# The gate weights load in twelve pieces, the first batches are turned in another order, and the last output tiles get buffers of their own

## The chip, the cores and the metric

The kernel runs on one core of one Trainium2 chip. The metric is the device time of one execution in microseconds (us). Three runs of the kernel before gave a median of 959.32 us (958.61 to 961.28).

## The reference

The input `x` is 32 batches of 128 rows by 512 columns. Each batch has a category; its 512 x 512 matrix and its bias are picked from 64. What follows is a gated feed-forward network with simulated quantisation:

```
c    = x @ W[cat] + b[cat]                       # per batch
c    = act_qdq(c)                                # 16-bit scale from max|c| over everything
up   = act_qdq(c @ lpbq(w_up).T)                 # 512 -> 1536
gate = act_qdq(c @ lpbq(w_gate).T)
gate = act_qdq(gate * u16(sigmoid(gate)))
o    = act_qdq(gate * up)
out  = x + o @ lpbq(w_down).T                    # 1536 -> 512
```

`lpbq` rounds weights to 4 bits with one scale for each block of 32 along the inner dimension. `act_qdq` needs the maximum over the whole tensor, so each stage must be complete before the next can be quantised.

## The kernel before, in words

Every engine has its instructions written out by hand; they meet at semaphores. The 32 batches are 8 chunks of 4 (`BPC`); in what follows a batch is numbered 0 to 31 and `r` is its place in its chunk.

**Conditioning stage (the first 139 us).** For each batch PE turns `x` with four transposes (`turn_x`, L750), ACT copies the result out of PSUM into `xt` (`copy_xt`, L537), PE multiplies with the batch's matrix in `w_ring` (`cond_matmul`, L760), and DVE adds the bias (`add_bias`, L1018). PE turns batch b+1 just ahead of multiplying batch b. `x_ring` and `w_ring` have four places each, so SP may issue the matrix of batch b (1 MB) only when the product of batch b-4 is done, and right behind it the `x` of batch b+1 (256 KB). Batches 0 and 1 are multiplied in halves of the contraction (`cond_halves`, L779), since their matrices come in two loads. Between the halves of batch 0 PE sums up the biases of all batches (eight small instructions into `bias_bank`) and turns batch 1 (`sum_bias_and_turn`, L812). Thirteen matmuls on zeros (`spare_matmuls`) fill PE's time before the first matrix is there.

**Weights beside it.** SP also loads `w_gate` into `wf` in four loads of 768 KB, behind the matrices of batches 7, 8, 9 and 11 (`load_chunk`, L393). DVE takes the maximum of each block of 32 of such a quarter (`gate_blocks`, L1055): quarter 0 after batch 11, quarters 1, 2, 3 after batches 12, 13, 14. `weight_steps` (three instructions, L977) follows after batch 14, and `weight_scale` (seven instructions on one column, L983) after batch 15; its last one signals `wscale_ready`. From chunk 4 on DVE quantises one slice of 512 columns ahead of each `add_bias` (`quantise_slice`, L1001, three instructions). ACT makes the upper part of each slice (`high_part`, L545). In chunk 4 ACT's order is: copy batch 16, copy batch 17, wait for `wscale_ready`, `high_part(0)`, copy batch 18, `high_part(1)`, copy batch 19, `high_part(2)` (`cond_chunk` of ACT, L569). ACT works strictly in this order, and PE's product of batch 18 needs the copy of batch 18.

**Gate and up projections, elementwise work, maxima.** From 142 to 644 us PE multiplies all chunks with both weights in float16 high and low parts; then DVE and ACT find the maximum of the product.

**Down projection (from 700 us).** Chunks alternate between two sets of four PSUM banks. PE multiplies a chunk in four quarters (`down_quarter`, L912), in each for four tiles `r`, each with nine matmuls of 512 columns. DVE finishes a tile (`finish_tile`, L1391: scale, and add `x` from `x_res`) into `y_out`; both have two places. SP stores it and loads the next `x_res` behind that (`finish_chunk`, L496). At the end SP waits for the stores to land.

## Time and profile before

| what | us |
|---|---|
| median of three runs | 959.32 |
| profiled execution, its own time | 959.35 |
| its span, first to last instruction | 957.5 |
| PE busy | 894.5 |
| DVE busy | 657.7 |
| ACT busy | 420.6 |
| conditioning stage, PE | 1.2 to 139 |
| PE idle between up and down projection | 643.7 to 700.0 |
| last matmul starts | 953.68 |

The profile lists for each engine when an instruction started and what ended the idle time ahead of it. The chain of waits goes back from the last instruction to whatever released each step; work on it counts one to one in the time, all else is hidden. PE has few idle stretches: 1.2 us at the start, 0.6 us ahead of the first product, three tenths at 142 us and the long one at 644 us. The duration of a matmul in a row contains the time until its result has drained, so rows overlap; the distance between starts is what a matmul costs in a stream.

### The profile page before, as it was taken

To read this page: it belongs to the slowest core of one execution; us is meant where nothing else is said; L and a number is where in the kernel's file an instruction comes from. 1 tells how busy PE (TensorE), PEld (TensorE's weight loads), DVE (VectorE), ACT (ScalarE), POOL (GpSimd) and SP (SyncE) were. 2 spreads that over 40 slices of the span, in tenths; PEclk is the share of its full clock that TensorE was granted. 3 is DMA by queue.
4 is the path that set the end of the run, shared out by engine and by line. 5 is a ranking of instruction groups with operands and counts; after the bars stand their busy time and mean duration, and the time that the engine had idled before them with its cause. 6 is when DMAs were issued, how large, how long until landed. Compare 5 with 4: busy or idle time off the path is not lost.

```text
span 957.5 us, 13113 instructions
## 1 busy us (share of the span) xinstructions
PE 894.5 (93%) x4736; PEld 477.7 (50%) x4736; DVE 657.7 (69%) x792; ACT 420.6 (44%) x454; POOL 3.1 (0%) x12
## 2 busy tenths in 40 slices
PE   9999999999999999999999999980079999999998
PEld 7999994444444444444444444430034444444443
DVE  2349869655667455279898889669999878855511
ACT  1112335223223232299798882229866444444000
POOL 0000000000000000000000000000000000000000
PEclk9999999999999999999999999995579999999999
DMA  9999862553574443689999735999978999977221
GB/s 334 405 393 325 324 242 100 165 164 122 165 253 131 141 132 121 220 304 419 407 388 391 261 125 207 407 422 414 418 272 317 320 339 348 331 272 282 88 88 66
DMA packets 81587, 254.32 MB, mean 266 GB/s; under 512 B 32082, under 2 KB 32082, under 8 KB 77714
## 3 DMA queue, kind: packets, MB, share of 16 engines
q1 hardware_dynamic: 46354, 198.72, 55.5%
q10 hardware_dynamic: 35200, 55.20, 16.4%
q8 instruction: 15, 0.25, 0.1%
q14 instruction: 18, 0.15, 0.0%
HBM read 173.94 MB, written 73.66 MB: 259 GB/s over the span
## 4 chain that ended last, share of the span: by engine, by line
PE 90%; DMA 4%; ACT 3%; issue 1%; DVE 1%; SPq 0%; ACTq 0%; POOL 0%; DVEq 0%
PE bank L857 16%; PE bank L858 16%; PE bank L859 16%; PE bank L771 11%; PE bank L892 6%; PE bank L894 6%; PE bank L893 6%; ACT umag L701 2%; DMA up_extra<-up_scratch 2%; PE bank L757 2%; PE bank L904 1%; PE bias_bank L892 1%; PE wt_bank L892 1%; PE wt_bank L893 1%; PE wt_bank L894 1%
## 5 line engine op out<-in xcount | busy, mean ns | idle before, releaser
L607 ACT ACTIVATE stage<-bank 128x512 f32<-128x512 f32 x186 | 108.5, 593 | 212.3 <-PE bank L859 161.2
L1135 DVE TENSOR_REDUCE tile_max<-stage 128x1 f32<-128x1536 f32 (+1 forms) x62 | 108.4, 1748 | 34.7 <-ACT stage L607 31.7
L857 PE MATMUL bank<-xq_head,wt_up 128*128 x336 | 127.4, 379 | 0.9 <-ACT stage L607 0.9
L857 PE MATMUL bank<-xq_head,wt_gate 128*128 (+1 forms) x336 | 127.4, 379 | 0.3 <-DVE xq_head L1122 0.3
L858 PE MATMUL bank<-xq_head,wt_up 128*128 x336 | 127.3, 379 | 0.0
L859 PE MATMUL bank<-xq_head,wt_up 128*128 x336 | 127.3, 379 | 0.0
L858 PE MATMUL bank<-xq_head,wt_gate 128*128 (+1 forms) x336 | 127.3, 379 | 0.0
L859 PE MATMUL bank<-xq_head,wt_gate 128*128 (+1 forms) x336 | 127.3, 379 | 0.0
L771 PE MATMUL bank<-xt,w_ring 128*128 128x128 f32 x960 | 112.1, 275 | 0.0
L771 PEld LDWEIGHTS bank<-xt,w_ring 128*128 128x128 f32 x960 | 109.9, 192 | 0.0
L1015 DVE SCALAR_TENSOR_TENSOR wparts<-wf,scal,wparts 128x512 f16<-128x512 f32 (+2 forms) x36 | 27.0, 749 | 62.9 <-ACT wparts L550 62.8
L1397 DVE SCALAR_TENSOR_TENSOR y_out<-bank,scal,x_res 128x512 f32<-128x512 f32 x24 | 17.9, 747 | 69.3 <-PE bank L894 66.8
L893 PE MATMUL bank<-wt_down,o_even 128*128 128x512 f16 x168 | 63.7, 379 | 0.0
L892 PE MATMUL bank<-wt_down,o_even 128*128 128x512 f16 x168 | 63.7, 379 | 0.0
L894 PE MATMUL bank<-wt_down,o_even 128*128 128x512 f16 x168 | 63.7, 379 | 0.0
L929 PE MATMUL bank<-wt_down 128*128 128x512 f16 x11 | 4.9, 630 | 56.3 <-DVE o_max L1329 56.3
L649 ACT ACTIVATE code<-gate_ring,scal 128x1536 int16<-128x1536 f32 x32 | 50.2, 1571 | 11.7 <-DMA wt_down<-wparts 6.8
L1329 DVE CUSTOM_DVE_ANT_0 junk<-act_codes,umag 128x1536 bf16<-128x1536 int16 x32 | 53.9, 1755 | 1.3 <-ACT umag L701 1.3
L1377 DVE SCALAR_TENSOR_TENSOR ocode<-act_codes,scal,ocode 128x1536 int16<-128x1536 int16 x30 | 54.3, 1810 | 0.4
L720 ACT ACTIVATE ocode<-up_ring,scal 128x1536 int16<-128x1536 f32 x31 | 48.4, 1561 | 11.6 <-DVE o_odd_head L1387 7.0
L857 PEld LDWEIGHTS bank<-xq_head,wt_up 128*128 128x128 f16 x336 | 32.9, 98 | 41.0 <-ACT stage L607 1.4
L857 PEld LDWEIGHTS bank<-xq_head,wt_gate 128*128 128x128 f16 x336 | 32.9, 98 | 40.4 <-DVE xq_head L1122 1.3
(205 smaller groups left out, 1354.4 us busy)
## 6 DMA issues: line engine op xcount, KB each, us to landing
up_ring<-up_scratch SPq DMA_DIRECT2D x54, 768.0 KB, 7.4
w_ring<-in_L_cond_W_dram SPq DMA_DIRECT2D x30, 1024.0 KB, 6.6
gate_scratch<-stage ACTq DMA_DIRECT2D x32, 768.0 KB, 3.4
gate_ring<-gate_scratch SPq DMA_DIRECT2D x32, 768.0 KB, 9.4
up_scratch<-stage ACTq DMA_DIRECT2D x30, 768.0 KB, 7.9
product_scratch<-prod_ring SPq DMA_DIRECT2D x19, 768.0 KB, 9.0
back_ring<-product_scratch SPq DMA_DIRECT2D x19, 768.0 KB, 13.0
gate_even<-gate_scratch SPq DMA_DIRECT2D x16, 768.0 KB, 8.0
```

Source lines behind the costliest of these rows:

```text
L607: nc.scalar.activation(stage[:, q % 2, n % PIECE_TILES, :], up_bank(i, n), ACT.Copy)\
L649: nc.scalar.activation(code[:, j % 2, :], gate_ring[:, j % RING, :], ACT.Copy, scale=k_g)\
L771: mm = nc.tensor.matmul(bank[:, m * S:(m + 1) * S], w_ring[:, r, k, m * P:(m + 1) * P], xt[:, r % 2, k, :], start=(k == 0), stop=(k == KH ...
L857: nc.tensor.matmul(bank, w_hi, x_hi, start=(k == 0), stop=False)
L858: nc.tensor.matmul(bank, w_hi, x_lo, start=False, stop=False)
L859: mm = nc.tensor.matmul(bank, w_lo, x_hi, start=False, stop=(k == KH - 1))
L892: nc.tensor.matmul(bank, o_hi, wt_down[:, 0, k, :], start=(k == 0), stop=False)
L893: nc.tensor.matmul(bank, o_hi, wt_down[:, 1, k, :], start=False, stop=False)
L894: return nc.tensor.matmul(bank, o_lo, wt_down[:, 0, k, :], start=False, stop=(k == NT - 1))
L1135: V.tensor_reduce(tile_max[:, side, bass.ds(Q * i + q, 1)], stage[:, q % 2, :, :].rearrange("p t c -> p (t c)"), AX.X, ALU.max, apply_abso ...
L1329: V.tensor_tensor_reduce(junk[:, k % 2, :], act_piece(max_piece(k)), umag[:, k % MSLOTS, :], 1.0, 0.0, ALU.mult, ALU.max, o_max[:, k:k + 1 ...
L1377: V.scalar_tensor_tensor(out=ocode[:, q % 2, :], in0=act_piece(n), scalar=k_o, in1=ocode[:, q % 2, :], op0=ALU.mult, op1=ALU.mult).then_in ...
```

## The change

Four things change.

1. `w_gate` is loaded in twelve loads of 256 KB, one behind the matrix of each of the batches 6 to 17 (`GATE_AT = 6`); each quarter has a semaphore. The loops over chunks 1 to 4 on SP are written out for this.
2. DVE takes the maxima of quarter 0 after batch 7, of quarter 1 after batch 10, of quarter 2 after batch 13, and of quarter 3 after batch 15. `weight_steps` follows behind quarter 3, after batch 15, and `weight_scale` after batch 16.
3. PE does the bias sum and the turn of batch 1 right behind the turn of batch 0, ahead of the first half of batch 0. The spare matmuls are nine, then three (eight, then five before). `halves_copied` now counts two copies, so that each of two PSUM banks is waited for by itself.
4. The last two output tiles have their own `x_tail` and `y_tail`, loaded by one 512 KB load well ahead. The last tile is computed as two halves of 256 columns in two banks (`last_quarter`): per quarter eighteen matmuls of 256 columns in the place of nine of 512. DVE finishes and SP stores each half by itself. PE's loop over pairs of chunks is one round shorter and the last two chunks are written out.

```diff
+GATE_AT = 6
...
+        x_tail = place("x_tail", R + 30 * K, [2, H], f32)
+        y_tail = place("y_tail", R, [2, H], f32)
...
-                    if r in gate_parts:
-                        at = SLICES * gate_parts[r]
-                        sp.dma_start(wf[:, at:at + SLICES, :], wg_view[:, at:at + SLICES, :]).then_inc(wgate_in, 16)
-
-            load_chunk(1, {3: 0})
-            load_chunk(2, {0: 1, 1: 2, 3: 3})
-            with sp.Fori(3, CHUNKS) as i:
-                load_chunk(i, {})
+                    if isinstance(i, int) and 0 <= BPC * i + r - GATE_AT < WSLICES:
+                        n = BPC * i + r - GATE_AT
+                        sp.dma_start(wf[:, n, :], wg_view[:, n, :]).then_inc(wgate_in[n // SLICES], 16)
+
+            for i in range(1, 5):
+                load_chunk(i)
+            with sp.Fori(5, CHUNKS) as i:
+                load_chunk(i)
...
+            sp.wait_ge(sgn_made, PIECES - 1)
+            sp.dma_start(x_tail[:, :, :], x_flat[B - 2:B, :, :].rearrange("a s d -> s a d")).then_inc(xtail_in, 16)
             finish_chunk(CHUNKS - 1, 0, True)
+            for n, (b, cols) in enumerate(((B - 2, slice(0, H)), (B - 1, slice(0, H // 2)), (B - 1, slice(H // 2, H)))):
+                sp.wait_ge(ytail_made, n + 1)
+                sp.dma_start(out[b, :, cols], y_tail[:, b - B + 2, cols]).then_inc(ytail_out[n], 16)
...
             pe.wait_ge(spare_made, 1)
-            spare_matmuls(8)
+            spare_matmuls(9)
...
-                        if r and m == 2:
-                            pe.wait_ge(halves_copied, 1)
+                        if r and m >= 2:
+                            pe.wait_ge(halves_copied, m - 1)
...
-                cond_halves(0, sum_bias_and_turn)
+                sum_bias_and_turn()
+                spare_matmuls(3)
+                cond_halves(0, None)
...
             turn_x(0, 0, True)
-            spare_matmuls(5)
             first_cond_chunk()
...
+                for half, bank in enumerate((down_bank(1, BPC - 1), down_bank(0, 0))):
+                    cols = slice(half * H // 2, (half + 1) * H // 2)
+                    for t in range(PIECE_TILES):
+                        k = PIECE_TILES * q + t
+                        o_hi, o_lo = (o_slot(1, q)[:, part, t, (BPC - 1) * P:BPC * P] for part in range(2))
+                        nc.tensor.matmul(bank[:, cols], o_hi, wt_down[:, 0, k, cols], start=(k == 0), stop=False)
+                        nc.tensor.matmul(bank[:, cols], o_hi, wt_down[:, 1, k, cols], start=False, stop=False)
+                        mm = nc.tensor.matmul(bank[:, cols], o_lo, wt_down[:, 0, k, cols], start=False, stop=(k == NT - 1))
+                    if q == Q - 1:
+                        mm.then_inc(right_done if half else left_done, 1)
...
             def in_chunk_3(r):
-                if r < 3:
-                    gate_blocks(r + 1)
-                if r == 2:
+                if r == 1:
+                    gate_blocks(2)
+                if r == 3:
+                    gate_blocks(3)
                     dve.wait_ge(wblocks_maxed, KH)
                     weight_steps(0, WG)
-                if r == 3:
-                    weight_scale(0, WG)
-
-            cond_chunk(1)
-            cond_chunk(2, None, lambda r: gate_blocks(0) if r == 3 else None)
+
+            cond_chunk(1, None, lambda r: gate_blocks(0) if r == 3 else None)
+            cond_chunk(2, None, lambda r: gate_blocks(1) if r == 2 else None)
             cond_chunk(3, None, in_chunk_3)
-            cond_chunk(4, 2)
+            cond_chunk(4, 2, lambda r: weight_scale(0, WG) if r == 0 else None)
...
+            for half, bank in enumerate((down_bank(1, BPC - 1), down_bank(0, 0))):
+                cols = slice(half * H // 2, (half + 1) * H // 2)
+                dve.wait_ge(right_done if half else left_done, 1)
+                V.scalar_tensor_tensor(out=y_tail[:, 1, cols], in0=bank[:, cols], scalar=k_y, in1=x_tail[:, 1, cols],
+                                       op0=ALU.mult, op1=ALU.add).then_inc(ytail_made, 1)
```

At the start of the program, behind the first spare matmul, PE's rows before the change are these (`spare` are the zeros, `ident` with `x_ring` a turn, `bias_rows` the bias sum, `w_ring` a product; in brackets stands what is waited for):

```order
L744 MATMUL bank<-spare 128x512 x7
L757 MATMUL bank<-ident_93,x_ring 128x128 [waits x_in0,ident_made]
L757 MATMUL bank<-ident_93,x_ring 128x128 x3
L744 MATMUL bank<-spare 128x512 x5
L792 MATMUL bank<-xt,w_ring 128x128 [waits w_head_in0,x_copied]
L792 MATMUL bank<-xt,w_ring 128x128 x5
L792 MATMUL wt_bank<-xt,w_ring 128x128 x2
L815 MATMUL bias_bank<-onehot,bias_rows 128x32 [waits onehot_made]
L815 MATMUL bias_bank<-onehot,bias_rows 128x32 x3
L757 MATMUL bank<-ident_93,x_ring 128x128 [waits x_in1]
L757 MATMUL bank<-ident_93,x_ring 128x128 x3
L792 MATMUL bank<-xt,w_ring 128x128 [waits w_in0]
```

And these are PE's rows at the start of the changed kernel:

```order
L758 MATMUL bank<-spare 128x512 [waits spare_made]
L758 MATMUL bank<-spare 128x512 x8
L771 MATMUL bank<-ident_95,x_ring 128x128 [waits x_in0,ident_made]
L771 MATMUL bank<-ident_95,x_ring 128x128 x3
L829 MATMUL bias_bank<-onehot,bias_rows 128x32 [waits onehot_made]
L829 MATMUL bias_bank<-onehot,bias_rows 128x32 x3
L771 MATMUL bank<-ident_95,x_ring 128x128 [waits x_in1]
L771 MATMUL bank<-ident_95,x_ring 128x128 x3
L758 MATMUL bank<-spare 128x512 x3
L806 MATMUL bank<-xt,w_ring 128x128 [waits w_head_in0,x_copied]
L806 MATMUL bank<-xt,w_ring 128x128 x5
L806 MATMUL wt_bank<-xt,w_ring 128x128 x2
```

The four bias instructions and the turn that waits for `x_in1` stood between the two halves of batch 0 (`w_head_in0` and `w_in0`); now they stand ahead of both, with three spare matmuls behind them.

On DVE, at the end of chunk 3 before the change (`wstep` to `wrecip` are the weight steps, `scal` on one column is the scale, `cond_head` is a bias addition, that of batch 15 here, `cond_max` the maximum of a chunk):

```order
L979 TENSOR_SCALAR wstep<-wstep 128x192 [waits wblocks_maxed]
L980 RECIPROCAL wrecip<-wstep 128x192 [waits scalar_step]
L981 TENSOR_REDUCE scal<-wstep 128x1 [waits scalar_step]
L1029 TENSOR_TENSOR cond_head<-bank,bias 128x4x128 [waits cond_done]
L987 TENSOR_SCALAR scal<-scal 128x1 [waits all_max]
L988 TENSOR_SCALAR scal<-scal 128x1 [waits scalar_step]
L989 TENSOR_SCALAR scal<-scal 128x1 [waits scalar_step]
L990 TENSOR_SCALAR scal<-scal 128x1 [waits scalar_step]
L991 TENSOR_SCALAR scal<-scal 128x1 [waits scalar_step]
L993 TENSOR_SCALAR scal<-scal 128x1 [waits scalar_step]
L995 COPY scal<-scal 128x1 [waits scalar_step]
L1045 TENSOR_REDUCE cond_max<-cond_head 128x1 [waits cond_copied]
```

And DVE from the maxima of quarter 3 on in the changed kernel, where the first bias addition is that of batch 16:

```order
L1101 TENSOR_REDUCE wstep<-wf 128x48 [waits wgate_in3]
L1022 TENSOR_SCALAR wstep<-wstep 128x192 [waits wblocks_maxed]
L1023 RECIPROCAL wrecip<-wstep 128x192 [waits scalar_step]
L1024 TENSOR_REDUCE scal<-wstep 128x1 [waits scalar_step]
L1088 TENSOR_REDUCE cond_max<-cond_head 128x1 [waits cond_copied]
L1048 TENSOR_TENSOR wf<-wf,wrecip 128x512
L1050 TENSOR_SCALAR wf<-wf 128x512 [waits w_scaled]
L1052 TENSOR_TENSOR wf<-wf,wstep 128x512 [waits w_rounded]
L1072 TENSOR_TENSOR cond_head<-bank,bias 128x4x128 [waits cond_done]
L1030 TENSOR_SCALAR scal<-scal 128x1 [waits all_max]
```

The weight steps moved behind batch 15, and the scale moved past the chunk's maximum, the quantising of slice 0 and the bias addition of batch 16.

## Rows read from the trace of the kernel before

**Rows 1.** The page, the chain that ended last, by engine:

```profile
PE 90%; DMA 4%; ACT 3%; issue 1%; DVE 1%; SPq 0%; ACTq 0%; POOL 0%; DVEq 0%
```

**Rows 2.** Timeline, PE, from 1 us (start us, length us, engine, line, operation):

```profile
1.16 3.60 PE L744 MATMUL bank<-spare 128*128 128x512 f16 x8 [1.16 <-DVE spare L955]
...
4.84 1.10 PE L757 MATMUL bank<-ident,x_ring 128*128 128x128 f32 x4
...
5.74 1.46 PE L744 MATMUL bank<-spare 128*128 128x512 f16 x5
```

**Rows 3.** Chain that ended last, to 25 us (start us, us until the next):

```profile
7.83 1.58 PE bank L792 x12
...
9.86 1.00 PE bias_bank L815 x8
...
11.54 1.34 PE bank L792 x12
...
19.80 3.57 PE bank L771 x32
```

**Rows 4.** Tile w_ring, the load of batch 3, issued at 8.58 us:

```profile
DMA to landing us min/median/max: 11.3/11.3/11.3
```

**Rows 5.** Chain that ended last, 47 to 56 us:

```profile
50.02 0.48 PE bank L757 x4
...
54.14 0.74 PE bank L757 x4
```

**Rows 6.** Tile x_ring, loads issued from 40 to 60 us:

```profile
DMA to landing us min/median/max: 7.0/9.4/10.7
```

**Rows 7.** DMA view, 40 to 60 us:

```profile
DMA packets 2250, 8.21 MB, mean 410 GB/s; under 512 B 192, under 2 KB 192, under 8 KB 1600
```

**Rows 8.** Timeline, DVE, 71 to 82 us:

```profile
71.26 1.74 DVE L1058 TENSOR_REDUCE wstep<-wf 128x48 f32<-128x1536 f32 x1
73.03 0.26 DVE L979 TENSOR_SCALAR wstep<-wstep 128x192 f32<-128x192 f32 x1
...
74.98 0.68 DVE L1029 TENSOR_TENSOR cond_head<-bank,bias 128x512 f32<-128x512 f32 x1
75.58 0.14 DVE L987 TENSOR_SCALAR scal<-scal 128x1 f32<-128x1 f32 x1
...
76.77 2.28 DVE L1045 TENSOR_REDUCE cond_max<-cond_head 128x1 f32<-128x2048 f32 x1
78.96 0.68 DVE L1005 TENSOR_TENSOR wf<-wf,wrecip 128x512 f32<-128x512 f32 x1
...
80.75 0.68 DVE L1029 TENSOR_TENSOR cond_head<-bank,bias 128x512 f32<-128x512 f32 x1
```

**Rows 9.** Timeline, ACT, 80 to 82 us:

```profile
80.93 0.72 ACT L550 ACTIVATE wparts<-wf,scal 128x512 f16<-128x512 f32 x1 [5.15 <-DVE wf L1009]
81.56 0.58 ACT L542 ACTIVATE xt<-bank 128x512 f32<-128x512 f32 x1
```

**Rows 10.** Timeline, PE: turn of batch 17, product of batch 18:

```profile
74.50 0.64 PE L757 MATMUL bank<-ident,x_ring 128*128 128x128 f32 x4
...
83.09 3.74 PE L771 MATMUL bank<-xt,w_ring 128*128 128x128 f32 x32
```

**Rows 11.** Timeline, PE, the last matmul:

```profile
953.68 0.38 PE L894 MATMUL bias_bank<-wt_down,o_odd_tail 128*128 128x512 f16 x1
```

**Rows 12.** Chain that ended last, from 951 us:

```profile
951.43 2.73 DMA x_res<-in_x_dram
...
954.24 0.75 DVE y_out L1397
```

**Rows 13.** Timeline, DVE, a bias addition of 128 columns out of PSUM:

```profile
13.44 0.35 DVE L1023 TENSOR_SCALAR cond_head<-bank,bias 128x128 f32<-128x128 f32 x1 [2.25 <-PE wt_bank L792]
```

**Rows 14.** Windows (us, busy of PE, PEld, DVE, ACT, POOL; granted clock; DMA; GB/s):

```profile
647.00:648.00 1.00, 0.00 (x0) 0.00 (x0) 0.69 (x1) 1.00 (x2) 0.00 (x0) 0.93 1.02 418
...
705.00:706.00 1.00, 1.00 (x4) 0.39 (x3) 0.93 (x3) 0.00 (x0) 0.00 (x0) 0.55 1.00 406
```

More of the change, by code:

```diff
@@ L269, in sem @@
             return ctx.enter_context(nc.semaphore(name))
-        idx_in, bias_in, wgate_in, wup_in = sem("idx_in"), sem("bias_in"), sem("wgate_in"), sem("wup_in")
+        idx_in, bias_in, wup_in = sem("idx_in"), sem("bias_in"), sem("wup_in")
+        wgate_in = [sem(f"wgate_in{m}") for m in range(KH)]
         w_in = [sem(f"w_in{n}") for n in range(BPC)]
@@ L316, in adaln_ffn @@
         y_out_done = [sem(f"y_out_done{n}") for n in range(2)]
+        xtail_in, ytail_made = sem("xtail_in"), sem("ytail_made")
+        ytail_out = [sem(f"ytail_out{n}") for n in range(3)]
+        left_done, right_done = sem("left_done"), sem("right_done")
         ky_made = sem("ky_made")
@@ L391, in _, with load_chunk @@
                     load_x_batch(0, r + 1, True)
[L393 removed]
+            def load_chunk(i):
                 for r in range(BPC):
@@ L496, in finish_chunk @@
             def finish_chunk(i, pairs_left, last):
-                for r in range(BPC):
+                for r in range(BPC // 2 if last else BPC):
                     if r < pairs_left:
@@ L508, in finish_chunk @@
                                  y_out[:, r % 2, :]).then_inc(y_out_done[r % 2], 16)
-                    if not last or r < 2:
+                    if not last:
                         load_x(BPC * i + r + 2, r)
@@ L515, in _ @@
             finish_chunk(CHUNKS - 2, 0, False)
+            sp.wait_ge(sgn_made, PIECES - 1)
+            sp.dma_start(x_tail[:, :, :], x_flat[B - 2:B, :, :].rearrange("a s d -> s a d")).then_inc(xtail_in, 16)
             finish_chunk(CHUNKS - 1, 0, True)
+            for n, (b, cols) in enumerate(((B - 2, slice(0, H)), (B - 1, slice(0, H // 2)), (B - 1, slice(H // 2, H)))):
+                sp.wait_ge(ytail_made, n + 1)
+                sp.dma_start(out[b, :, cols], y_tail[:, b - B + 2, cols]).then_inc(ytail_out[n], 16)
             for r in range(2):
-                sp.wait_ge(y_out_done[r], 16 * B // 2)
+                sp.wait_ge(y_out_done[r], 16 * (B - 2) // 2)
+            for n in range(3):
+                sp.wait_ge(ytail_out[n], 16)
         @block.gpsimd
@@ L922, in down_quarter, with last_quarter @@
                     mm.then_inc(piece_used, 1)
+            def last_quarter(q):
+                pe.wait_ge(o_ready, PIECES - Q + q + 1)
+                for r in range(BPC - 1):
+                    if q == 0:
+                        pe.wait_ge(y_made, BPC * (CHUNKS - 3) + r + 1)
+                    for t in range(PIECE_TILES):
+                        mm = down_tile(1, q, r, t)
+                    if q == Q - 1:
+                        mm.then_inc(out_done, 1)
+                if q == 0:
+                    pe.wait_ge(y_made, BPC * (CHUNKS - 2) + 1)
+                for half, bank in enumerate((down_bank(1, BPC - 1), down_bank(0, 0))):
+                    cols = slice(half * H // 2, (half + 1) * H // 2)
+                    for t in range(PIECE_TILES):
+                        k = PIECE_TILES * q + t
[3 more added lines that the diff above has]
+                        mm = nc.tensor.matmul(bank[:, cols], o_lo, wt_down[:, 0, k, cols], start=False, stop=(k == NT - 1))
+                    if q == Q - 1:
+                        mm.then_inc(right_done if half else left_done, 1)
+                if q < Q - 1:
+                    mm.then_inc(piece_used, 1)
             for j in range(SLICES):
@@ L935, in _ @@
                         down_quarter(h, h, q, True)
-            with pe.Fori(1, CHUNKS // 2) as pair:
+            with pe.Fori(1, CHUNKS // 2 - 1) as pair:
                 for h in range(2):
@@ L939, in _ @@
                         down_quarter(2 * pair + h, h, q, False)
+            for q in range(Q):
+                down_quarter(CHUNKS - 2, 0, q, False)
+            for q in range(Q):
+                last_quarter(q)
         @block.vector
@@ L1424, in _ @@
             down_pair(CHUNKS // 2 - 1, False, True)
-            for h in range(2):
-                for r in range(BPC):
-                    finish_tile(CHUNKS - 2 + h, r, h, False)
+            for r in range(BPC):
+                finish_tile(CHUNKS - 2, r, 0, False)
+            for r in range(2):
+                finish_tile(CHUNKS - 1, r, 1, False)
+            dve.wait_ge(out_done, B - 1)
+            dve.wait_ge(xtail_in, 16)
+            V.scalar_tensor_tensor(out=y_tail[:, 0, :], in0=down_bank(1, 2), scalar=k_y, in1=x_tail[:, 0, :],
+                                   op0=ALU.mult, op1=ALU.add).then_inc(ytail_made, 1)
[3 more added lines that the diff above has]
+                V.scalar_tensor_tensor(out=y_tail[:, 1, cols], in0=bank[:, cols], scalar=k_y, in1=x_tail[:, 1, cols],
+                                       op0=ALU.mult, op1=ALU.add).then_inc(ytail_made, 1)
 _INS = ['x', 'itok_B_0_63', 'L0_cond_W', 'L0_cond_b', 'L0_ffn_w_gate', 'L0_ffn_w_up', 'L0_ffn_w_down']
```

5 lines of the change are left out of this document (2 added, 3 removed).

## The prediction

> **What bounds the kernel now.** I read the page's chain first: PE holds 90% of it [rows 1], so what counts is where PE is later or earlier than its own stream of instructions. Then the timeline and the chain at both ends of the program, the landing of the loads that PE turns and multiplies, and DVE and ACT around 71 to 84 us, since the change touches these. The reader is to see four things. At the start PE's own work sets the time from 7.83 us on [rows 3]. In the conditioning stage a batch costs PE 4.05 us (0.48 for a turn, 3.57 for 16 matmuls as 32 rows of f32 halves) [rows 3, 5], and everything else hides behind it, once excepted [rows 5]. ACT's copy of batch 18 is only 0.95 us ahead of PE: it ends at 81.56 + 0.58 = 82.14, PE needs it at 83.09 [rows 9, 10]. And after the last matmul [rows 11] the rest is serial: one wait for a load, a DVE instruction, a store [rows 12].
>
> **Part 1, the start.** Between the halves of batch 0 stand the bias sum and a turn, 9.86 to 11.54: 1.68 us go from there [rows 3]. They now stand ahead. Eight spare matmuls from 1.16 took 3.60, so 0.45 each, and a ninth moves the turn of batch 0 from 4.84 to about 5.05. That turn issues in 0.90 (to 5.74) [rows 2]: 5.95. The bias sum adds 1.00, the turn of batch 1 the 0.68 left of the 1.68 [rows 3]: 7.63. Three spare matmuls at about 0.22 (five took 1.46 with a slow first one and the drain [rows 2]) give 8.28, against 7.83: 0.45 later. In return the first half of batch 0, 2.03 us before (7.83 to 9.86), should take 1.79, half of the 3.57 of a full batch [rows 3], since PE no longer idles ahead of it: 0.24. Sum: 1.68 - 0.45 + 0.24 = 1.47 us gained. Bounds: nothing, if the moved work runs on the slow clock of the first microseconds or a load is late; 1.9 if all of it fits ahead of 7.83. The split of `halves_copied` lets PE wait for one DVE copy instead of two; a copy lasts 0.35 [rows 13], of which I count nothing. What is late next is the matrix of batch 3: issued at 8.58, landed 11.3 later at 19.88 [rows 4]. Its product began 1.79 behind 19.80, at 21.59 [rows 3], and would now begin at 20.12. That just fits.
>
> **Part 2, the gate loads.** Before, the `x` of batch 12 was issued at 43.28 behind three megabytes of gate weights and took 10.7 us [rows 6], to 53.98. PE's turn at 54.14 came 4.12 after the last one at 50.02 and took 0.74 instead of 0.48 [rows 5]: 0.07 + 0.26 = 0.33 us lost, which the spread loads give back. At that point only six slices (1.6 MB) instead of 3.1 MB have gone ahead; at 410 GB/s [rows 7] that is 3.8 us less queue, while PE comes 1.8 earlier. One batch (1.31 MB) with one slice (0.26 MB) takes 3.85 us at 410 GB/s [rows 7] against PE's 4.05, so the queue does not grow. The eight more DMA issues on SP stand ahead of the next `x` load each time; SP waits for PE in every batch, and that wait hides them. Bounds: 0.33 gained; nothing gained.
>
> The Trainium skill's page "DMA: Bandwidth & Descriptors" (Bandwidth, Measured) asks for DMAs of 1 MiB or more and so speaks against cutting four loads into twelve; its fit in Anatomy of one DMA has about 2 us of fixed cost each. Laid end to end that would make a batch with its slice longer than PE's 4.05, and PE would wait. The trace has 256 KB loads mixed with 1 MB ones at 410 GB/s [rows 7], so the costs overlap here and I give this little weight (a rival below).
>
> **Part 3, the weight scale.** This is the dearest part. Times are from the end of batch 15's product, E = 74.50 before [rows 10]. Turns are 4.05 apart, so that of batch 16 was at 70.45, and DVE's maxima at 71.26 [rows 8] came 0.81 behind the product's end (bias addition in between). DVE in the changed order: maxima of quarter 3 start at E + 0.81; +1.77 (71.26 to 73.03) weight steps; +1.95 (to 74.98) chunk maximum; +2.19 (76.77 to 78.96) quantise slice 0; +1.79 (to 80.75) add bias 16; +0.60 (74.98 to 75.58) scale; +1.19 (to 76.77) and 0.08 to its end [rows 8]: `wscale_ready` at E + 10.38. Before, it came at about E + 2.35, and ACT waited for slice 0 instead, to E + 6.43 = 80.93 [rows 9]. ACT then needs 0.10 to start, 0.63 for `high_part(0)` and 0.58 for the copy of batch 18 [rows 9]: E + 11.69, with a hop to PE 11.75. PE wants it at 83.09 - 74.50 = 8.59 [rows 10]. So PE stands idle for 3.16 us. Behind ACT's wait are queued the copies of batches 18 and 19; the second comes at about E + 13.4, PE asks for it at 11.75 + 4.05, so it costs nothing more. DVE reaches bias 18 when PE has finished it, as before, and from there the stage has its old rhythm; nothing gives the 3.16 back, since the end of the stage is again PE. Slice 11 goes out behind the matrix of batch 17, when batch 13's product ends: E - 8.10, 64.6 with the 1.8 us gained so far, and 0.7 for SP's three issues, 65.3; with the 7.0 us that the last load of rows 6 took it is there by 72.5, DVE asks at 74.50 - 1.80 + 0.81 = 73.5. Bounds: 2.2 (if the DVE steps close up) to 4.5 (if slice 11 is a microsecond late). That the earlier maxima (after batches 7, 10, 13) move into idle time of DVE is free.
>
> **Part 4, the end.** PE's stream ends as before; eighteen matmuls of 256 columns per quarter for nine of 512 may add a few nanoseconds each, 0.08 in all (an estimate; bounds 0 to 0.3). The last tile waited for `x_res`: issued 951.43, 2.73 on the way, 954.16 [rows 12], while PE was done at 953.68 + 0.38 = 954.06 [rows 11]; with `x_tail` loaded long ahead 0.10 goes. DVE's 0.75 for 512 columns [rows 12] and 0.35 for 128 [rows 13] give 0.48 for 256: 0.27 less. The left half runs under PE's right half. The last store carries 131 KB less, 0.32 at 410 GB/s [rows 7]. Together 0.10 + 0.27 + 0.32 - 0.08 = 0.61 gained; bounds 0.1 (the store's time is all latency) and 0.8.
>
> **Sum.** 959.35 (the profiled execution, practically the median 959.32) - 1.47 - 0.33 + 3.16 - 0.61 = 960.1 us.
>
> **Rivals.** *A, no stall*: ACT or DVE gets there in time and the gains stand alone: 959.35 - 1.47 - 0.33 - 0.61 = 956.9. For it: the sum of parts 1, 2, 4 is solid; against it: seven DVE steps in a fixed order with measured lengths, and ACT's strict order. 11%. *B, the clock falls in the stall* (the slower side): PE stopped at 643.7, and the granted clock was 0.93 in the mean of 647 to 648, so it fell at about 647.9, 4.2 us later; PE began again at 700.0, and the mean of 0.55 from 705 to 706 says it was back at 705.9 [rows 14]. 5.9 us at 1.2 instead of 2.4 GHz cost 3.0: 963.1. It decides if the clock has fallen by the time the copy of batch 18 is there; my stretch is 3.2 us, shorter than the 4.2 of that row, which speaks against. 13%. The Trainium skill warns, in "TensorE: Matmul & The Clock Gate" (Why this matters for your kernels), against idle gaps of a few microseconds between bursts of matmuls; by that rule B would be the likelier case. *C, nothing gained at the start*: clock late for the moved work, or batch 3's matrix late: 961.5. 10%. *D, the twelve loads are too slow* and PE waits for them, 0.2 us or more in each of twelve batches: 962.5 and above. 4%. The forecast has 62%.
>
> **How the numbers follow.** A measurement of this kernel tells about 0.3%, 2.9 us, from no change: faster is below 956.4, slower above 962.2. The forecast's own range, from the bounds that are likely together, is 959.0 to 961.3: no change. A lies at the edge inside, and somewhat under half of it (with the upper bounds of parts 1 and 4) below: faster 6 to 8%. B mostly and D are slower: 14%. The range that holds 8 in 10 takes in most of A and the near part of B: 956.8 to 962.6.
>
> **What would show it.** `wscale_ready`'s copy instruction at 83.0 or so; ACT's `high_part(0)` waiting for that instruction and no longer for L1009's successor; an idle stretch of about 3 us of PE ahead of batch 18 with the copy as releaser, and a granted clock of 1.00 behind it. Batch 3's product at 20.1; no longer turn at batch 12; a last DVE instruction of about 0.48. The prediction is wrong if PE has no gap near 81 us, if the clock falls there, or if PE waits for a load at 16 to 20 us.

## The result, and the profile after it

| | before | changed |
|---|---|---|
| median of 11 executions, same comparison | 960.60 us | 962.67 us |
| lowest to highest | 958.61 to 961.41 | 962.19 to 964.10 |
| profiled execution (its span) | 959.35 (957.5) | 962.19 (960.3) |
| its mean granted clock | 0.970 | 0.970 |

The medians differ by 2.07 us. The ratio of the two kernels is 1.0025, with a 95% interval of 1.0015 to 1.0035, which is 2.4 us: slower, and the interval leaves no change out. The forecast was 960.1, 0.75 above its base of 959.35, and called no change, with a range up to 962.6. The measured 962.67 lies just above that range. Of the 2.57 us between forecast and measured time 1.25 are not the change's: in this comparison the kernel before itself took 960.60 and not 959.35. The other 1.3 us are what the change cost more than forecast, and they are what has to be explained.

First the profiled execution. Its chain that ended last (start us, us until the next) up to 25 us, which answers to [rows 3]:

```profile
3.75 7.88 DMA w_ring<-in_L_cond_W_dram
...
11.68 1.60 PE bank L806 x12
...
19.98 0.48 PE bank L771 x4
20.46 3.57 PE bank L785 x32
```

The full product that began at 19.80 before begins at 20.46: the start is 0.66 us later, not 1.47 earlier. PE had done its early work in time. Its timeline (start us, us, engine, line, operation, idle before and releaser):

```profile
1.16 4.02 PE L758 MATMUL bank<-spare 128*128 128x512 f16 x9 [1.16 <-DVE spare L998]
...
5.27 1.04 PE L771 MATMUL bank<-ident,x_ring 128*128 128x128 f32 x4
...
6.34 1.07 PE L829 MATMUL bias_bank<-onehot,bias_rows 64*128 64x32 f32 x8
```

What came late is a load: the second half of batch 0's matrix was issued at 3.75 and landed 7.88 us later. In the traces of the kernel before and of all experiments below it took 5.1 to 6.0 us. So this is something of this execution and not of the change, and the experiments have to say what the start is worth. PE waited 1.2 us for it, which is about half of what this execution lost at the start: in e4, the same code there, this product begins at 18.32, 2.14 earlier. The rest is no single wait.

PE's own waits (engine, line, waited for: us in total, times, longest) show that load and the stall that part 3 of the prediction described:

```profile
PE bank L785 <- ACT xt L556: 3.0, 1, 3.0
...
PE bank L806 <- DMA w_ring<-in_L_cond_W_dram: 1.2, 1, 1.2
```

The timeline of DVE, which answers to [rows 8]:

```profile
74.98 0.69 DVE L1072 TENSOR_TENSOR cond_head<-bank,bias 128x512 f32<-128x512 f32 x1 [3.36 <-PE bank L785]
75.58 1.74 DVE L1101 TENSOR_REDUCE wstep<-wf 128x48 f32<-128x1536 f32 x1
77.36 0.26 DVE L1022 TENSOR_SCALAR wstep<-wstep 128x192 f32<-128x192 f32 x1
...
79.31 2.27 DVE L1088 TENSOR_REDUCE cond_max<-cond_head 128x1 f32<-128x2048 f32 x1
81.51 0.68 DVE L1048 TENSOR_TENSOR wf<-wf,wrecip 128x512 f32<-128x512 f32 x1
...
83.29 0.68 DVE L1072 TENSOR_TENSOR cond_head<-bank,bias 128x512 f32<-128x512 f32 x1
83.89 0.14 DVE L1030 TENSOR_SCALAR scal<-scal 128x1 f32<-128x1 f32 x1
...
85.01 0.15 DVE L1038 COPY scal<-scal 128x1 f32<-128x1 f32 x1
```

ACT, which answers to [rows 9], and PE, which answers to [rows 10]:

```profile
85.20 0.72 ACT L564 ACTIVATE wparts<-wf,scal 128x512 f16<-128x512 f32 x1 [9.14 <-DVE scal L1038]
85.83 0.58 ACT L556 ACTIVATE xt<-bank 128x512 f32<-128x512 f32 x1
```

```profile
74.78 0.64 PE L771 MATMUL bank<-ident,x_ring 128*128 128x128 f32 x4
...
82.88 0.64 PE L771 MATMUL bank<-ident,x_ring 128*128 128x128 f32 x4
86.53 3.83 PE L785 MATMUL bank<-xt,w_ring 128*128 128x128 f32 x32 [3.01 <-ACT xt L556]
```

E, the time of 74.50 before, is 74.78 here. The scale is ready at 85.16, E + 10.38, and the product of batch 18 starts at E + 11.75: both to the hundredth as forecast. In this execution the granted clock stayed up behind the gap (window from 86 us; us, busy of PE, PEld, DVE, ACT, POOL; granted clock; DMA share; GB/s):

```profile
86.00:87.00 1.00, 0.47 (x4) 0.48 (x5) 0.96 (x3) 0.42 (x2) 0.00 (x0) 1.00 1.08 422
87.00:88.00 1.00, 1.00 (x12) 1.00 (x11) 1.00 (x2) 1.00 (x2) 0.00 (x0) 1.00 0.89 352
```

At the end, which answers to [rows 11, 12], PE and DVE:

```profile
957.36 0.27 PE L957 MATMUL bank<-wt_down,o_odd_tail 128*128 128x256 f16 x1
957.67 0.48 DVE L1478 SCALAR_TENSOR_TENSOR y_tail<-bank,scal,x_tail 128x256 f32<-128x256 f32 x1 [0.50 <-PE bank L957]
```

From the start of the last DVE instruction to the end of the span it is 2.63 us now and was 3.26 (957.5 - 954.24).

The balance of the two profiled executions, read at the same three places: the start +0.66 (20.46 - 19.80); from there to E -0.38 (74.78 - 74.50 is 0.28), the longer turn and waits of batches 10 and 12 that are gone; from E to the product of batch 18 +3.16 (86.53 - 83.09 is 3.44); the rest -0.60. Together +2.84, which is 962.19 - 959.35.

That balance explains this one execution, and not the median. It had the clock at 0.970 on average, which is the highest of the 11 (four have it), and a late load by chance. The other seven executions had a mean clock of 0.966 or 0.968. In 107 undisturbed executions of the kernel before, run beside the experiments, one was below 0.970. So the first theory is: **the stall of 3 us lets TensorE's clock fall in most executions** (rival B of the prediction), and parts 1, 2 and 4 gain what was forecast. The main rivals: part 1 gains nothing, because the first matrix comes late (SP's loop written out, or the loads' order); and the twelve loads cost time by themselves.

### The profile page after: what moved, and what is told of

Read it like the earlier page. It is cut to its first block, busy times and chain, and to the rows that moved or that the text cites. A ratio compares the mean times of both kernels' runs of the same rounds, so it can differ in the third digit from the quotient of the medians.

```text
span 960.3 us, 13140 instructions
## 1 busy us (share of the span) xinstructions
PE 894.4 (93%) x4771; PEld 481.1 (50%) x4771; DVE 657.8 (68%) x793; ACT 420.9 (44%) x454; POOL 3.1 (0%) x12
## 4 chain that ended last, share of the span: by engine, by line
PE 89%; DMA 4%; ACT 3%; issue 2%; DVE 2%; SPq 0%; ACTq 0%; POOL 0%; DVEq 0%
PE bank L872 16%; PE bank L873 16%; PE bank L874 16%; PE bank L785 10%; PE bank L908 6%; PE bank L907 6%; PE bank L909 6%; ACT umag L715 2%; DMA up_extra<-up_scratch 2%; PE bank L771 1%; PE bank L919 1%; PE wt_bank L908 1%; PE wt_bank L907 1%; PE wt_bank L909 1%; DMA wt_down<-wparts 1%
```

## The experiments

Each time is a median, beside the median of the kernel before on the same chip. The ratios behind the times are not the quotients of these medians, and differ from them by up to 0.9 us.

### One part at a time

**e1: part 4 alone** (parts 1 to 3 undone).

```diff
-                sum_bias_and_turn()
-                spare_matmuls(3)
-                cond_halves(0, None)
+                cond_halves(0, sum_bias_and_turn)
...
-            for i in range(1, 5):
-                load_chunk(i)
-            with sp.Fori(5, CHUNKS) as i:
-                load_chunk(i)
+            load_chunk(1, {3: 0})
+            load_chunk(2, {0: 1, 1: 2, 3: 3})
+            with sp.Fori(3, CHUNKS) as i:
+                load_chunk(i, {})
```

> The kernel before with part 4 alone (own buffers for the last two tiles, the last tile in halves). Theory (the prediction's part 4): 0.6 us faster than before, 0.1 to 0.8. Rival (the store's time is all latency and the written-out chunks cost PE time): no gain, the last DVE instruction shorter by 0.27 but the span not. In the profile: last DVE instruction 0.48 us, from its end to the end of the span about 0.3 us less than before.

958.32 beside 958.86, ratio 0.9993 (0.9984 to 1.0002). The timeline at the end:

```profile
953.06 0.27 PE L955 MATMUL bank<-wt_down,o_odd_tail 128*128 128x256 f16 x1
953.37 0.48 DVE L1477 SCALAR_TENSOR_TENSOR y_tail<-bank,scal,x_tail 128x256 f32<-128x256 f32 x1 [0.50 <-PE bank L955]
```

The last two matmuls of 256 columns start 0.11 apart, so one of 512 would have started at 952.95. From there to the end of the span (956.1) it is 3.15 us, against 3.82 before (957.5 - 953.68): 0.67 gained, where the forecast has 0.61. The median's 0.5 agrees but is too small to be told from nothing.

**e2: part 1 alone** (loads of `w_gate`, DVE's order and the end as before).

```diff
-            cond_chunk(1, None, lambda r: gate_blocks(0) if r == 3 else None)
-            cond_chunk(2, None, lambda r: gate_blocks(1) if r == 2 else None)
+            cond_chunk(1)
+            cond_chunk(2, None, lambda r: gate_blocks(0) if r == 3 else None)
             cond_chunk(3, None, in_chunk_3)
-            cond_chunk(4, 2, lambda r: weight_scale(0, WG) if r == 0 else None)
+            cond_chunk(4, 2)
```

> The kernel before with part 1 alone (bias sum and turn of batch 1 ahead of batch 0, nine and three spare matmuls). Theory S (the changed order itself makes PE wait for the second half of batch 0's matrix and costs what the profile after shows there): batch 3's product begins at about 22.2 us instead of 21.6, time 0.5 to 1 us above before. Rival L (the order gains 1.5 us as predicted, and the late landing in the profile after, 11.6 instead of 8.95 us, was the luck of one execution): batch 3's product at 20.1 to 20.6 us, time 1 to 1.5 us below before.

958.67 beside 958.86, ratio 1.0000 (0.9991 to 1.0009): nothing. But the chain shows the gain, and where it goes:

```profile
18.03 3.57 PE bank L777 x32
...
33.13 12.34 DMA x_ring<-in_x_dram
...
45.51 0.75 PE bank L763 x4
...
53.98 0.74 PE bank L763 x4
```

The product that began at 19.80 before begins at 18.03, 1.77 us earlier. At 45.51 the gain is nearly used up: the `x` of that batch, issued at 33.13, was 12.34 us on the way behind the gate weights, and the turn took 0.75. The turn at 53.98 stands against 54.14 in [rows 5]. An earlier start is worth nothing while the loads behind it are late. Part 2 is what turns it into time. Neither theory written down for e2 had this: one expected a later start, the other 1 to 1.5 us in the time.

**e3: parts 2 and 3 alone** (start and end as before).

```diff
-            spare_matmuls(9)
+            spare_matmuls(8)
...
-                sum_bias_and_turn()
-                spare_matmuls(3)
-                cond_halves(0, None)
+                cond_halves(0, sum_bias_and_turn)
```

> The kernel before with parts 2 and 3 alone (twelve loads of 256 KB, maxima and scale moved). Theory (the stall of part 3 behind ACT's wait for the weight scale, less the wait of batch 12 that goes): +3.2 - 0.3 = 2.8 us slower than before, one gap of 3.0 to 3.3 us of PE ahead of batch 18's product. Rival (the slower start is caused by the loop over chunks 1 to 4 written out on SP or by the loads, not by the order on PE): the second half of batch 0's matrix lands at 11 us or later here too, and the time is 4 us or more above before.

964.12 beside 958.86, ratio 1.0046 (1.0032 to 1.0060), and all 5 executions below 0.970. PE's timeline and the windows:

```profile
86.03 5.44 PE L778 MATMUL bank<-xt,w_ring 128*128 128x128 f32 x32 [3.01 <-ACT xt L549]
```

```profile
86.00:87.00 1.00, 0.97 (x4) 0.97 (x5) 1.00 (x3) 0.51 (x1) 0.00 (x0) 0.51 0.96 369
...
88.00:89.00 1.00, 1.00 (x7) 1.00 (x7) 0.97 (x3) 0.13 (x1) 0.00 (x0) 0.50 0.23 96
89.00:90.00 1.00, 1.00 (x9) 1.00 (x9) 0.50 (x1) 0.59 (x1) 0.00 (x0) 0.79 0.13 49
```

Here the clock is at half, 1.2 of 2.4 GHz, from the moment PE resumes, and the product takes 5.44 us instead of the 3.83 it took without a fall. That is most of why the loss is 4.4 us (by the ratio) to 5.3 (by the medians) and not the 2.8 expected. The second half of batch 0's matrix was 5.4 us on the way although SP's loop is written out here as in the changed kernel: that rival is false.

### Taking the stall away

**e4: everything but the stall.** ACT copies batch 18 before it waits for the scale:

```diff
-                    if weights == 1 and r == 1:
-                        act.wait_ge(wscale_ready, 1)
-                    if weights is not None and r >= weights:
-                        high_part(0, BPC * (i - 4) + r - 1, BPC * (i - 4) + r - 1, 0)
+                    if weights == 1 and r == 2:
+                        act.wait_ge(wscale_ready, 1)
+                        high_part(0, 0, 0, 0)
+                    elif weights == 1 and r == 3:
+                        high_part(0, 1, 1, 0)
+                        high_part(0, 2, 2, 0)
+                    elif weights == 0:
+                        high_part(0, BPC * (i - 4) + r - 1, BPC * (i - 4) + r - 1, 0)
```

> The changed kernel with ACT's order alone altered in chunk 4: the copy of batch 18 comes ahead of the wait for the weight scale, high parts 0, 1, 2 behind the copies of batches 18 and 19. Theory (the stall is ACT's strict order): no gap of PE ahead of batch 18, 3.2 us less than the changed kernel, so about 0.8 us below the kernel before. Rival (DVE itself is too late there and PE then waits for a bias addition instead): a gap of 1 us or more ahead of batch 20, less than 2 us gained on the changed kernel.

956.26 beside 958.86, ratio 0.9973 (0.9963 to 0.9982), none of 10 executions below 0.970. Its chain:

```profile
18.32 3.57 PE bank L789 x32
...
40.37 0.48 PE bank L775 x4
...
44.42 0.48 PE bank L775 x4
...
48.48 0.48 PE bank L775 x4
...
52.53 0.48 PE bank L775 x4
```

The product of batch 3 starts at 18.32 + 1.79 = 20.11, where the prediction has 20.12, and the turns from 40 to 53 us are 4.05 or 4.06 apart: the twelve loads cost PE nothing. ACT now waits 5.10 us instead of 9.14, behind the copy:

```profile
83.06 0.72 ACT L564 ACTIVATE wparts<-wf,scal 128x512 f16<-128x512 f32 x1 [5.10 <-DVE scal L1042]
```

The prediction's rival A, all gains and no stall, is 956.9 - 959.35 = -2.4 us; e4 has -2.6. So parts 1, 2 and 4 were sized right together, and part 3 with what follows it is the whole loss. **e15** is the same kernel on another chip.

> The changed kernel with ACT's order altered, again: every execution at a mean clock of 0.970 or 0.971, ratio to before 0.9965 to 0.998, 3.2 us (the stall) below e14 and 4 to 5 below e13.

956.66 beside 958.85, ratio 0.9986 (0.9975 to 0.9997), 1 of 12 executions below 0.970. It gains less than e4 by the ratio because three executions at a mean clock of 0.970 took 959.88 to 960.12, and e7 below has two of the kind (959.80 and 959.98). None of these has a trace.

**e7: the scale earlier instead** (slices from batch 5 on, maxima and scale one batch earlier, as far as they follow from it):

```diff
-GATE_AT = 6
+GATE_AT = 5
...
+                if r == 3:
+                    weight_scale(0, WG)
...
-            cond_chunk(4, 2, lambda r: weight_scale(0, WG) if r == 0 else None)
+            cond_chunk(4, 2)
```

> The changed kernel with every slice of w_gate and its maxima one batch earlier (behind batches 5 to 16; maxima after batches 6, 9, 12, 14, steps after 14, scale after 15 as before the change). Theory (twelve loads are harmless, only the scale's place costs): no gap ahead of batch 18, 3.2 us and the clock's part less than the changed kernel, 2.6 us below before, like the kernel with ACT's order altered. Rival D (small loads crowd the queue when they begin earlier): PE waits for x or a matrix between batches 5 and 12, 0.3 us or more in sum, above the kernel with ACT's order altered.

956.45 beside 958.79, ratio 0.9981 (0.9970 to 0.9991), 0 of 12, and no gap ahead of batch 18. Two quite different edits that remove the gap give the same time.

**e10: e4 without part 1** (the edit shown for e3, made on e4).

> The changed kernel with ACT's order altered and without part 1 (bias sum and turn of batch 1 back between the halves of batch 0). Theory (part 1 is worth 1.5 us once the spread loads of part 2 let PE keep it; alone it was given back at the turns of batches 9, 10 and 12): 0.9 to 1.0 us below before (0.33 and 0.6), 1.5 us above the kernel with ACT's order altered. Rival (the gain came from parts 2 and 4, part 1 is worth nothing): the same time as with it, 2.4 us below before.

957.37 beside 958.79, ratio 0.9985 (0.9976 to 0.9995). It is 1.4 us below the kernel before, where e4 is 2.6 and e15 is 2.2 below in their medians. So part 1 is worth 1.2 or 0.8 us of the 1.47, and by the ratio of e15 (0.9986) nothing. The three ran on three chips: the medians don't settle it, and the size of part 1 rests on the traces.

**e8: e4 without the three spare matmuls** ahead of the first half batch.

```diff
                 sum_bias_and_turn()
-                spare_matmuls(3)
                 cond_halves(0, None)
```

> The changed kernel with ACT's order altered as before and without the three spare matmuls ahead of the first product. Theory: the first product begins when its half matrix is there (7.7 to 8.0 us) instead of 8.2 us: 0.2 to 0.5 us less than with them. Rival: PE's clock is no longer kept up for the first product, which then takes longer than 1.8 us: no gain or 0.5 us and more lost.

956.53 beside 958.79, ratio 0.9978 (0.9969 to 0.9987): the same as e4, where 0.2 to 0.5 us less was expected. The first product starts at 8.06 instead of 8.19, the bias sum takes 1.31 us in the place of 1.0:

```profile
6.04 1.31 PE bias_bank L833 x8
```

### A stall, but shorter or filled

**e9: DVE's chunk maximum (2.27 us) moved from ahead of the scale to behind batch 17's bias addition.**

```diff
...
-            cond_chunk(4, 2, lambda r: weight_scale(0, WG) if r == 0 else None)
+            def in_chunk_4(r):
+                if r == 0:
+                    weight_scale(0, WG)
+                if r == 1:
+                    chunk_max(3)
+
+            cond_chunk(4, 2, in_chunk_4)
```

The lines left out make chunk 3 itself leave its maximum out.

> The changed kernel with DVE's maximum of chunk 3 (2.19 us) moved from ahead of the weight scale to behind the bias addition of batch 17. Theory (DVE's steps in order, added up, set ACT's wait, and the clock falls only in a long gap): a gap of 3.0 - 2.2 = 0.8 us of PE ahead of batch 18, mean clock 0.970 or 0.971 in every execution, time 0.8 to 1.0 us above the kernel with ACT's order altered, so 1.4 to 1.8 us below before. Rival (any gap there brings the clock down): executions with a mean clock of 0.966 to 0.968 remain.

957.25 beside 958.79, ratio 0.9985 (0.9976 to 0.9994), 0 of 11 executions below 0.970:

```profile
82.57 3.61 PE L785 MATMUL bank<-xt,w_ring 128*128 128x128 f32 x30 [0.85 <-ACT xt L556]
```

With 0.85 us of gap the kernel is still faster than before. The gap has shrunk by 2.16 of the 2.27 that were moved, so the chain of DVE steps in the prediction is the one that counts.

**e6, e11, e14: PE works on zeros in the stall** (the output isn't touched; chunk 4 of PE's loop is written out for it). e6 and e14 are the same kernel, with 12 matmuls; e11 has 14.

```diff
+                    if isinstance(i, int) and i == 4 and r == 2:
+                        for _ in range(12):
+                            nc.tensor.matmul(bias_bank[:, :], spare[:, 0:P], spare[:, :], start=True, stop=True)
...
-            with pe.Fori(1, CHUNKS - 1) as i:
+            with pe.Fori(1, 4) as i:
+                cond_chunk(i, False, False)
+            cond_chunk(4, False, False)
+            with pe.Fori(5, CHUNKS - 1) as i:
```

> The changed kernel with twelve matmuls on zeros (2.6 us) in the stall ahead of batch 18's product, chunk 4 written out on PE; the stall itself stays. Theory K: the clock stays at 1.00 there in every execution, mean clock 0.970 or above throughout, time 1 to 2 us below the changed kernel and closer together. Rival R: no difference to the changed kernel, 0.3 us at most.

> The changed kernel with fourteen matmuls on zeros (3.0 us) in the stall instead of twelve. Theory K (the clock falls because PE idles): no execution below a mean clock of 0.970, 1 to 2 us below the changed kernel. Rival (what fell to 0.968 in two executions with twelve was not the stall): executions of 0.968 remain with fourteen.

> The same with the twelve matmuls on zeros in the stall. Theory K: at most two in eleven executions below 0.970, median 1 to 2 us below e13. Rival: no difference.

e6: 960.55 beside 958.79, ratio 1.0021 (1.0010 to 1.0032), 2 of 9 executions below 0.970. e11: 960.83 beside 958.79, 1.0026 (1.0014 to 1.0039), 1 of 9. e14: 960.73 beside 958.85, 1.0020 (1.0011 to 1.0028), 1 of 11. For e6 and e11 no execution below 0.970 was expected, so with filling some are left, and two more matmuls did not change that. PE in e14:

```profile
81.41 2.75 PE L851 MATMUL bias_bank<-spare 128*128 128x512 f16 x12
84.51 1.72 PE L785 MATMUL bank<-xt,w_ring 128*128 128x128 f32 x13 [0.34 <-ACT xt L556]
```

**e13: e14 without its matmuls**, the fair partner, made from it so:

```diff
-                        for _ in range(12):
+                        for _ in range(0):
```

> The changed kernel with chunk 4 written out on PE and nothing in the stall: the control to e14. Theory K (the stall brings PE's clock down in part of the executions): half or more of the executions with a mean clock below 0.970, median 1 us or more above e14. Rival (filling does nothing): same share of executions below 0.970 and the same median as e14.

963.11 beside 958.85, ratio 1.0045 (1.0029 to 1.0061), 8 of 10 below 0.970. e13 and e14 differ only in what PE does in the gap, ran on the same chip, and differ by 2.4 us, with intervals that don't overlap. Batch 18 comes at 84.57 and 84.51, so the gap is equally long: **what PE does in the gap is worth 2.4 us, and brings the executions below 0.970 from 8 of 10 to 1 of 11.** The trace of e13 shows the fall:

```profile
84.00:85.00 1.00, 0.43 (x3) 0.44 (x4) 0.96 (x3) 0.51 (x2) 0.00 (x0) 1.00 1.03 389
85.00:86.00 1.00, 1.00 (x8) 1.00 (x7) 1.00 (x3) 0.91 (x2) 0.00 (x0) 0.58 0.86 354
```

By the turn behind batch 18 (89.87 against 88.18) the fall has cost 1.7 us. So not all of the 2.4 need be the fall itself: the two traces also differ in a later wait (next sentences) and in the clock at the down projection ("A second draw", below). e14 is 1.9 us above the kernel before, where the forecast's sum with a clock that holds is 0.8. Some 0.6 of the 1.1 between stand at PE's one wait for ACT's stage copy, behind 150 us: 1.5 to 1.7 us in the filled kernels and 2.5 in e13, against 1.0 in the changed kernel and 0.9 in the kernel before (a wait that the list of idle stretches ahead of the prediction leaves out). Whether the written-out code does that wasn't followed up.

### The changed kernel again

> The changed kernel once more, as it is, beside the next three. Theory K (PE's clock falls in the 3 us stall ahead of batch 18 in part of the executions): about 2.2 us above before, executions spread over some 3 us in steps with their mean clock (0.966 to 0.970), and if the profiled one has 0.968 or less, windows at 86 to 90 us with a granted clock of 0.5. Rival R (the spread is the landing of the first matrices): the mean clock doesn't go with the time, and the first products are later in slow executions.

> The changed kernel as it is, on the same chip as the three others, since its executions spread. Theory K: 2 to 4 us above before, most executions with a mean clock of 0.966 to 0.968, these 1 to 2.5 us slower than those at 0.970. Rival: the mean clock and the time do not go together.

**e5**: 962.17 beside 958.79, ratio 1.0043 (1.0030 to 1.0056), 4 of 5 executions below 0.970. The profiled one held the clock (0.971), had no late matrix, and took 959.12: 0.3 above the median before, where the forecast says 0.8. The four others took 961.78 to 964.17. **e12**, on another chip: 960.41 beside 958.79, ratio 1.0012 (1.0002 to 1.0021), 3 of 11 below 0.970, where 2 to 4 us and most executions were expected. Its profiled execution is one of the three, and shows the fall. PE:

```profile
80.95 0.64 PE L771 MATMUL bank<-ident,x_ring 128*128 128x128 f32 x4
84.60 1.68 PE L785 MATMUL bank<-xt,w_ring 128*128 128x128 f32 x11 [3.01 <-ACT xt L556]
```

and the windows:

```profile
84.00:85.00 1.00, 0.40 (x3) 0.41 (x4) 0.96 (x3) 0.47 (x1) 0.00 (x0) 1.00 1.04 410
85.00:86.00 1.00, 1.00 (x10) 1.00 (x9) 1.00 (x3) 0.95 (x2) 0.00 (x0) 0.88 0.97 363
86.00:87.00 1.00, 1.00 (x7) 1.00 (x6) 0.93 (x3) 0.26 (x1) 0.00 (x0) 0.50 0.34 127
...
88.00:89.00 1.00, 1.00 (x6) 1.00 (x6) 0.06 (x1) 0.16 (x1) 0.00 (x0) 0.50 0.04 16
89.00:90.00 1.00, 1.00 (x10) 1.00 (x9) 0.00 (x0) 0.00 (x0) 0.00 (x0) 0.91 0.00 0
```

PE stopped at about 81.6 and was back at 84.60 with a full clock. These rows show a granted clock of 1.00 or 0.50, and means between where it changed: the mean of 0.88 from 85 to 86 us says that the clock fell at about 85.8, when PE had been busy for 1.2 us, and it came back at about 89.2. The rows show 7, 7 and 6 matmuls a microsecond where there are 10 to 12 at full clock; the product took 5.46 us in all, against 3.83 with the clock up: 1.63 lost here. In e13 the same reading gives a fall at about 85.2, 0.6 us after PE resumed, and in e3 it came as PE resumed; all three came back 3.4 us after the fall.

**A second draw at the down projection.** PE stands idle once more, from about 644 to 700 us, in every kernel here. The traces show that the clock is not the same there from execution to execution either. e2, then e5:

```profile
645.00:646.00 1.00, 0.00 (x0) 0.00 (x0) 0.86 (x6) 0.59 (x1) 0.00 (x0) 0.78 1.02 418
```

```profile
704.00:705.00 1.00, 1.00 (x5) 0.34 (x4) 0.82 (x3) 1.00 (x2) 0.07 (x1) 0.67 0.64 154
```

In e2 PE's last matmul ended at 643.46 and the clock fell at about 645.6, 2.1 us later; over the 17 traces it is 2.1 to 5.4 us, and the 4.2 of [rows 14] is one of them. In e5 PE resumed at 701.77 and the clock was back at about 704.7, 2.9 us later; over the 17 traces it is 2.8 (e14) to 6.0 us (e3), with 5.9 in the kernel before and 5.7 in the changed kernel's first trace. The late return costs time: from there to the last matmul it is 252.4 us at least and 253.7 at most, and e5 has 252.55, the first trace of the changed kernel 253.79. That is 1.2 of the 3.07 us between these two executions of one kernel (959.12 and 962.19); the other 1.9 were lost ahead of batch 18, at the start. So the mean clock of an execution and its time also carry this draw, which the change doesn't touch.

### Taken together

| PE ahead of batch 18 | kernels | executions below a mean clock of 0.970 |
|---|---|---|
| stands 3 us | changed kernel, e3, e5, e12, e13 | 27 of 42 |
| works on zeros | e6, e11, e14 | 4 of 29 |
| stands 0.85 us or less | e1, e2, e4, e7 to e10, e15 | 2 of 89 |

The mean clock is taken over the whole program, so it doesn't say where the clock fell. That it fell behind the stall is seen in the traces of e3, e12 and e13; those of the changed kernel's first profile and of e5 show none there.

## Why the prediction was wrong

- **Part 3 and rival B: the step that failed.** The stall itself came as forecast (E + 10.38 and E + 11.75; 3.16 us). What failed is what the prediction made of it: "my stretch is 3.2 us, shorter than the 4.2 of that row, which speaks against". The 4.2 us of [rows 14] is when the clock fell in one execution. Over the 17 traces the same idle stretch has it after 2.1 to 5.4 us, and behind the stall it fell when PE was already back at work for 0.6 us in e13 and 1.2 us in e12. So a stretch of 3.2 us was not cleared by that row, and a fall was not over with once the copy of batch 18 was there. B got 13% and came in 27 of 42 executions of the kernels with the stall. The Trainium skill, "TensorE: Matmul & The Clock Gate" (Why this matters for your kernels), warns of gaps of a few microseconds: here it was the better guide. The runs agree with it in part: 27 of 42 executions, and not all.
- **What B costs.** B's price was 3.0 us, from a return 5.9 us after PE resumed. Behind the stall the clock was back after 3.4 us, and the product of batch 18 lost 1.6 us in e12, e13 and e3. So the price was put about twice too high for the fall itself. Larger differences stand beside it: 2.4 us between the medians of e13 and e14, and 3.6 between e5's four executions below 0.970 (962.77 on average) and the one without, whose clock also came back early at 704.7. The changed kernel's median is a mixture: 2.1, 3.4 and 1.6 us above the kernel before in three comparisons. No single sum could have given it.
- **What is not shown for the first comparison.** With its own base of 960.60 the forecast's sum is 961.35, and 962.67 was measured. Its four executions at a mean clock of 0.970 have a median of 962.3, its seven below one of 962.8. So only some 0.4 of the 1.3 us too much can be told from the mean clock, and all 11 executions lie above the sum. What the other microsecond is stays open; the one trace has the late load, and that only for itself.
- **Part 1** was right in size where it can act: the product of batch 3 at 20.11 for 20.12 in e4. The bias sum took 1.01 us at its new place there for 1.00, and the matrix of batch 3 was there in time, so rival C did not come. In the medians part 1 is worth between nothing and 1.2 us, which the runs don't narrow down. The prediction took it as worth 1.47 by itself; e2 shows that alone it is worth nothing, because the `x` loads behind the gate weights take it back by 54 us. In the sum this made no error, since part 2 comes with it. In the profiled execution of the changed kernel it is hidden, half of it by one late load.
- **Part 2** was right: 0.38 for 0.33, even turns in e4, and the argument from 410 GB/s against rival D held. The Trainium skill's advice of 1 MiB or more in "DMA: Bandwidth & Descriptors" (Bandwidth, Measured) doesn't show in this kernel: cutting four loads into twelve cost PE no wait in e4. (The page's figures are for loads issued from GpSimd, these are issued from SP.)
- **Part 4** was right: 0.67 in e1 for 0.61. The 0.60 behind batch 18 in the balance agrees, but holds the rest of the program too.
- **The range.** Its upper end, 962.6, was set in the near part of B, because B held 13%. With B at a half and at its price of 3.0 the middle of the forecast would have been 961.6, and the range would have taken in B's 963.1.

What stays open too: whether the clock falls varies from execution to execution, and its share from comparison to comparison (3 of 11 in e12, 8 of 10 in e13, which has chunk 4 written out), and no trace ahead of the gap was found to tell them apart; and why filling the gap left 4 of 29, which may be the second draw, since none of the four has a trace.

The best version is e4 (e15), below the kernel before by 2.6 and 2.2 us in the medians (2.6 and 1.3 by the ratios), with e7 as good.

## What to carry to other kernels

When a wait is moved on an engine that works strictly in order, list everything that is queued behind it and write out its time as here: the sum came out to a hundredth. Then give an idle gap on TensorE of 3 us its length and, as likely as not, some microseconds of half clock on top; a single row of a clock that fell after a longer gap doesn't clear a shorter one. A gain at the start counts only if the loads behind it keep up. And take the forecast's base from many executions: the kernel before had a median of 958.8 in four comparisons and 960.60 in another.

## What the hardware showed that was not expected

- The clock can fall after TensorE has resumed: in e12 it resumed at 84.60 and fell at about 85.8. It was back at about 89.2, 3.4 us later.
- In one and the same idle stretch behind 644 us the clock fell 2.1 to 5.4 us after TensorE's last matmul, and behind 700 us it was back 2.8 to 6.0 us after TensorE resumed, over 17 traces. The late return is worth some 1.2 us.
- The same code with the same gap of 3.0 us keeps the clock in some executions (959.12 in e5) and not in others (961.78 to 964.17).
- Zeros fed to PE through 2.75 of the 3 us keep the clock up in most executions: 8 of 10 had a mean clock below 0.970 without them and 1 of 11 with them on the same chip.
- The load of the second half of batch 0's matrix (512 KB), at the start of the program, took 5.1 to 6.0 us in every trace but one, and 7.88 in that one.
